# Rows of x gathered ahead for nine half units, their messages made from them later, and a table of counts turned round

## The chip, the cores and the metric

The kernel runs on one core of one Trainium2 chip. The metric is the device time in microseconds (us) of one launch; lower is better. The core has five engines with a queue each: TensorE (PE; PEld are its weight loads), VectorE (DVE), ScalarE (ACT), GpSimd (POOL) and SyncE (SP, which here only issues transfers). Each engine takes its own instructions in order and waits on semaphores.

## The reference, cut to what matters

6250 nodes with 128 features, 100000 edges sorted by `dst`, whose targets crowd at the low numbers. Per edge there are three attention weights, and one message that hangs on the source node alone:

```python
a_k = exp(relu(concat(h[src], h[dst]) @ W_att_k + b_att_k))          # k = 1, 2, 3
avg_a = (a1 / att1[dst] + a2 / att2[dst] + a3 / att3[dst]) / 3.0     # att_k = segment_sum(a_k, dst)
m = avg_a * relu(relu(relu(hs @ W_msg_1 + b1) @ W_msg_2 + b2) @ W_msg_3 + b3)
h_neigh = segment_sum(m, dst) / max(deg, 1)
out = relu(concat(h, h_neigh) @ W_c1 + b_c1) @ W_c2 + b_c2
x = layernorm(x + out)
```

## The kernel before, in words

**Prologue (0 to 54 us).** In 13 chunks of 512 nodes, PE, ACT and DVE make the message of every node (three layers) and its attention logits. A row of 131 words per node (128 of the message, 3 logits) is stored to `message_table` in HBM (`store_rows`). Meanwhile POOL and ACT write zeros into the accumulator `acc` and into `counts`, and no gather is issued, since the table isn't complete.

**The edge pass** then takes the edges in groups of 256 (two tiles of 128). The first 94 groups ("hot" ones, whose targets are the first 384 nodes) need no gather: 24 steps (`COUNT_STEPS`) count for each source node how often it meets each hot target, and 49 later steps (`HOT_AT` + 1 on, one block of 128 source nodes each) turn the counts into weighted sums. The other 297 groups are worked in 126 units: unit 0 of 4 tiles, units 1 to 23 of 8 tiles (the long ones, one beside each counting step), then 102 of 4 tiles (the last of 2). Each tile is gathered from `message_table` by one indirect DMA that POOL issues (L1154), 594 in all, into a ring of 8 places of 4 tiles; POOL may run ahead until the ring is full, and waits on `s_sum` then.

In step i each engine goes through a written order. DVE: `logits_of(i+1)` (L1634, then L1638, which waits until the rows of unit i+1 have landed), `add_counts(i-1)` (L1539, four a step), `one_hots(i)` (L1526, eight a step), `weights(i+1)` (L1646, L1651), `one_hot` (L1592), `add_sums(i-1)` (L1668). PE: `add_edges(i)` (L1281, L1285), `edge_q(i+2)` (L1267), `count_edges(i)` (L1302). ACT: `mask_copy(i+1)` (L1444), `exps(i+1)` (L1404), `low_hots(i)` (L1418, L1423). In a hot step (27 to 75) DVE has three `hot_weights` besides (L1561), ACT three exponentials (L1383) and three biased relus (L1374), PE eighteen matmul records (L1319). All three exponentials go through one bank of PSUM:

```python
act.wait_ge(s_hw, n)                                   # hot_exp: weights n-1 are done with the bank
act.activation(bank[EXP_BANK][0:m, 0:hot_nodes], hot_logit[0:m, n % TWO, :], ACT.Exp)
```

`counts` holds 16-bit counts, [source node in its block, block b, hot target d] with d innermost. `add_counts` adds a window of 6, 9 or 10 targets (`HOT_WIDTHS`, by cells of 32 groups) for all 49 blocks: 49 runs of w elements, in place. `hot_weights` reads the 384 targets of one block: one run.

From step 79 on, the final layers of the nodes (`final_pe`, `final_act`, `final_dve`: L836, L927, ...) lie between the units at places fixed by step numbers.

## Time and profile before

| | |
|---|---|
| time, median of 3 runs | 826.16 us (826.0 to 827.2) |
| the profiled execution: its own time / span | 826.97 / 822.9 us |
| busy: PE / DVE / ACT / POOL | 656.1 / 577.4 / 381.7 / 590.9 us |
| mean granted clock of TensorE | 0.809 |
| gathers on POOL | 594 |

An engine's busy time leaves out waits and the issue of plain transfers. "x" numbers are instructions. A matmul of 32-bit operands shows as two records. A name in brackets behind a row of the timeline is the idle time before it and what ended that. "issue" is idle time that nothing in the profile ended.

### The profile page before, as it was taken

Reading aid. Unit: us, or ns where it says so; the run is one execution under the profiler, and the core shown is the slowest. Engines: PE = TensorE matmul, PEld = TensorE weight load, DVE = VectorE, ACT = ScalarE, POOL = GpSimd, SP = SyncE. Lnnn points to the kernel's source line nnn. Section 1 sums busy time; section 2 is a strip of 40 time slices with the busy share of each in tenths; the row PEclk is TensorE's granted clock in tenths of the full one; section 3 lists DMA queues with packets and bytes.
Section 4 is the critical chain, followed back from the end, with each engine's and each line's share of the span. In section 5 each row is a group of like instructions: output and inputs, shape, how many; then the busy total and the mean of one; then the engine's idle time right before and its main releaser. Section 6 shows DMA issues by size and latency. Waiting matters only on the chain.

```text
span 822.9 us, 16893 instructions
## 1 busy us (share of the span) xinstructions
PE 656.1 (80%) x4917; PEld 512.9 (62%) x4917; DVE 577.4 (70%) x1934; ACT 381.7 (46%) x999; POOL 590.9 (72%) x638
## 2 busy tenths in 40 slices
PE   9945677777578778989898988888877978878885
PEld 5734455544345446778787877776666766667664
DVE  4882656585688877677776767775577868787766
ACT  5522555463444443677676767662123322333323
POOL 7437777777777777777777777777777777777770
PEclk9975555567565675799999999999699989998989
DMA  6533222225652233333333333334233443443421
GB/s 190 142 105 69 63 65 65 65 65 57 71 65 62 62 92 78 74 87 76 80 82 75 83 78 84 77 77 131 65 90 102 112 108 102 104 130 101 98 58 35
DMA packets 79474, 70.44 MB, mean 86 GB/s; under 512 B 34040, under 2 KB 65312, under 8 KB 79376
## 3 DMA queue, kind: packets, MB, share of 16 engines
q0 software_dynamic: 19008, 39.88, 22.2%
q1 hardware_dynamic: 60080, 29.28, 13.3%
q8 instruction: 42, 0.69, 0.3%
q14 instruction: 56, 0.46, 0.2%
q10 hardware_dynamic: 288, 0.13, 0.1%
HBM read 62.32 MB, written 6.90 MB: 84 GB/s over the span
## 4 chain that ended last, share of the span: by engine, by line
POOL 35%; DVE 21%; issue 19%; PE 17%; ACT 4%; DMA 2%; DVEq 2%; ACTq 0%; SPq 0%; POOLq 0%
POOL work L1154 34%; DVE fin L1561 4%; PE bank L1281 4%; DVE acc L1668 3%; ACT bank L1383 3%; DVE counts L1539 2%; DVE fin L1526 2%; DVE fin L927 2%; PE bank L836 2%; PE bank L565 2%; PE bank L544 2%; DMA work<-message_table,src_t 1%; PE bank L1285 1%; PE bank L1319 1%; DVE side L1592 1%
## 5 line engine op out<-in xcount | busy, mean ns | idle before, releaser
L1154 POOL DMA_INDIRECT work<-message_table,src_t x594 | 566.4, 953 | 191.8 <-issue 178.0
L1281 PE MATMUL bank<-work 128*128 128x144 f32 (+8 forms) x1188 | 248.7, 343 | 66.5 <-DVE acc L1668 66.4
L1281 PEld LDWEIGHTS bank<-work 128*128 128x128 f32 x1188 | 197.7, 234 | 100.4 <-issue 86.0
L1444 ACT COPY work<-bank 128x192 f32<-128x192 f32 (+7 forms) x126 | 37.4, 297 | 250.9 <-DVE work L1634 246.5
L1319 PE MATMUL bank<-work,fin 128*128 128x129 f32 (+1 forms) x882 | 117.3, 290 | 0.0
L1668 DVE TENSOR_TENSOR acc<-acc,bank 128x192 f32 (+8 forms) x297 | 88.7, 299 | 31.3 <-issue 7.5
L1319 PEld LDWEIGHTS bank<-work,fin 128*128 128x128 f32 (+1 forms) x882 | 108.2, 201 | 2.5 <-issue 0.6
L1383 ACT ACTIVATE bank<-hot_logit 128x384 f32<-128x384 f32 (+1 forms) x147 | 72.7, 494 | 70.9 <-DVE fin L1561 62.0
L1651 DVE TENSOR_TENSOR work<-bank,work 128x576 f32<-128x576 f32 (+7 forms) x126 | 86.2, 684 | 13.1
L1285 PE MATMUL bank<-work 128*4 128x48 f32 (+8 forms) x1188 | 95.0, 207 | 0.0
L1561 DVE SCALAR_TENSOR_TENSOR fin<-bank,counts 128x384 f32<-128x384 f32 (+1 forms) x147 | 81.4, 554 | 18.1 <-ACT bank L1383 17.4
L1302 PE MATMUL bank<-fin 128*128 128x294 bf16 (+2 forms) x188 | 63.7, 506 | 35.6 <-DVE fin L1526 20.4
L1374 ACT ACTIVATE hot_logit<-logits_or_x,work 128x384 f32<-128x384 f32 (+1 forms) x147 | 88.3, 600 | 0.0
L1638 DVE TENSOR_TENSOR work<-work 128x12 f32<-128x12 f32 (+1 forms) x126 | 22.2, 176 | 80.5 <-DMA work<-message_table,src_t 70.6
L836 PE MATMUL bank<-rest_w,acc 128*128 128x128 f32 x294 | 48.0, 324 | 34.2 <-DVE fin L927 29.3
L1285 PEld LDWEIGHTS bank<-work 128*4 128x4 f32 x1188 | 50.0, 88 | 38.3 <-issue 8.5
L1539 DVE TENSOR_TENSOR counts<-counts,bank 128x294 f32 (+2 forms) x94 | 57.4, 611 | 22.4 <-DVE counts L1539 12.8
L836 PEld LDWEIGHTS bank<-rest_w,acc 128*128 128x128 f32 x294 | 42.4, 227 | 36.5 <-DVE fin L927 30.6
L1302 PEld LDWEIGHTS bank<-fin 128*128 128x128 bf16 x188 | 22.5, 125 | 63.6 <-ACT fin L1423 30.7
L1418 ACT ACTIVATE fin<-fin 128x128 bf16<-128x128 f16 x188 | 59.3, 386 | 1.2 <-PE bank L1302 1.2
L1404 ACT ACTIVATE work<-work 128x12 f32<-128x12 f32 (+1 forms) x126 | 26.8, 213 | 65.4 <-DVE work L1638 63.7
L1646 DVE TENSOR_SCALAR work<-work 128x12 f32<-128x12 f32 (+1 forms) x126 | 24.5, 194 | 41.7 <-ACT work L1404 40.4
(132 smaller groups left out, 688.9 us busy)
## 6 DMA issues: line engine op xcount, KB each, us to landing
work<-message_table,src_t POOLq DMA_INDIRECT x594
side<-near_nodes SPq DMA_DIRECT2D x102, 48.0 KB
side<-logit_parts SPq DMA_DIRECT2D x297, 0.8 KB
message_table<-work SPq DMA_DIRECT2D x12, 262.0 KB, 3.4
work<-message_table SPq DMA_DIRECT2D x48, 65.5 KB
work<-in_x_t SPq DMA_DIRECT2D x12, 256.0 KB, 3.3
fin<-in_x SPq DMA_DIRECT2D x11, 256.0 KB, 2.9
logits_or_x<-in_x_t SPq DMA_DIRECT2D x11, 256.0 KB
```

The lines of the kernel that those rows point to most:

```text
L836: last = pe.matmul(to[:, k * P:(k + 1) * P], acc[:, k, nodes], wc1[:, 1, :], start=True, stop=True)
L1154: pool.indirect_dma_start(out=rows_of(n)[:, t, :], out_offset=None, in_=table[:, :], in_offset=bass.IndirectOffsetOnAxis(ap=src_t[:, h, g: ...
L1281: pe.matmul(sums[:, at:at + HEADS * w], rows_here[:, t, 0:P], wt_of(i)[:, t, :], start=h == 0, stop=h == TILES - 1)
L1285: last = pe.matmul(sums[SUMS_AT:SUMS_AT + HEADS + 1, at + HEADS * w:at + HEADS * w + w], a_col[:, i % THREE, t, :], mask_of(i)[:, t, :], s ...
L1302: pe.matmul(bank[COUNT_BANKS[g % FOUR]][:, 0:n], hot_lo[:, t % HOT_RING, :], hot_comb[:, t % HOT_RING, 0:n], start=h == 0, stop=h == TILES ...
L1319: last = pe.matmul(bank[SIDE_BANKS[h]][:, k * (P + 1):(k + 1) * (P + 1)], hot_wt[0:m, b % THREE, k, h * P:(h + 1) * P], rows_here, start=F ...
L1374: act.activation(hot_logit[0:m, n % TWO, :], hot_ld[0:m, k, :], ACT.Relu, bias=hot_block[0:m, b % BLOCKS, 1 + P + k:2 + P + k]).then_inc(s ...
L1383: act.activation(bank[EXP_BANK][0:m, 0:hot_nodes], hot_logit[0:m, n % TWO, :], ACT.Exp).then_inc(s_he, 1)
L1539: dve.tensor_tensor(here, here, bank[COUNT_BANKS[g % FOUR]][:, 0:w * n_blocks].rearrange("p (b d) -> p b d", d=w), ALU.add).then_inc(s_cad ...
L1561: dve.scalar_tensor_tensor(hot_wt[0:m, b % THREE, k, :], bank[EXP_BANK][0:m, 0:hot_nodes], FLT_MAX, counts[0:m, b, :], ALU.min, ALU.mult). ...
L1651: dve.tensor_tensor(wt_of(i).rearrange("p t (k w) -> p t k w", w=w), from_q(i)[:, :, PARTS:PARTS + w].unsqueeze(2).to_broadcast([P, n, HEA ...
L1668: dve.tensor_tensor(here, here, sums[:, at:at + (HEADS + 1) * w].rearrange("p (k w) -> p k w", w=w), ALU.add).then_inc(s_acc, 1)
```

## The change: what it does

For nine of the long units (4, 6, ..., 20) the second half, two groups, is no longer gathered in the edge pass. In the prologue POOL gathers rows of `x` for them (36 indirect DMAs of 128 rows, three staging buffers), SP stores each half unit to `early_table` in HBM (nine stores) and loads it back in steps 0, 2, ..., 16 (nine loads). The messages of these edges are made then, over two steps and a bit: PE turns the rows (`turn_early`), ACT copies them, PE and ACT run two layers, PE the third, DVE adds the bias into the ring (`rows_early`), ACT applies relu. PE adds the logits of their sources in `edge_q` (four small products). All of it uses bank 3, so that all long units share bank 1 for `edge_q`, which therefore waits for `weights` of the unit just before, and moves behind `count_edges`.

POOL no longer writes zeros for `counts` and for most of `acc`: it writes 5200 words. ACT writes 1000 words per chunk in place of 766, eight late pieces of `acc` (7016 words) behind the prologue's last relu, and the 9408 words of `counts` (five pieces) behind its first `exps`.

`counts` is held with the block b innermost. `add_counts` then touches one run of 49 w elements, and `hot_weights` reads 384 elements that lie 49 elements (98 bytes) apart. The index of the one-hots is made in 6 chained steps in place of 8.

```diff
 
 
 class Straight:
...
+    early_groups = [first_order[n][pair:] for n in early_units]
+    early_a, early_b = early_groups[0][0], early_groups[-1][-1] + 1
+    assert n_hot <= early_a
     columns_most = max(len(u) * TILES * width_of(g) for u in first_order + again_order for g in u)
     assert (HEADS + 1) * columns_most <= 512 * TILES
 
@@ -151,7 +159,7 @@
...
         tally_sum = fin[:, at_index:at_index + max(HOT_WIDTHS)]
         at_index += max(HOT_WIDTHS)
         same = fin[:, at_index:at_index + GROUP // 2].bitcast(bf16)
-        assert at_index + GROUP // 2 <= FIN
...
+        staged = [logits_or_x[:, 0:COLS], work[:, WORK - COLS:WORK], hot_logit_flat[:, 0:COLS]]
+        early_h, early_x, EARLY_BANK = staged[2], staged[1], 3
...
+        ACT_WORDS, POOL_FIRST, POOL_LAST = 1000, 2000, 3200
+        act_from = POOL_FIRST + POOL_LAST
+        late_from = act_from + n_chunks * ACT_WORDS
+        late_pieces = [(a, min(a + ACT_WORDS, n_zeros)) for a in range(late_from, n_zeros, ACT_WORDS)]
+        count_words = hot_nodes * n_blocks // 2
+        count_pieces = [(a, min(a + 2 * ACT_WORDS, count_words)) for a in range(0, count_words, 2 * ACT_WORDS)]
+        zeroed = 2 + n_chunks + len(late_pieces) + len(count_pieces)
...
+                STORE_AT = {0: [0], 2: [1], 3: [2], 5: [3], 6: [4], 8: [5], 10: [6], n_chunks - 1: [7, 8]}
+                assert [k for ks in STORE_AT.values() for k in ks] == list(range(EARLY))
...
+                    sp.wait_ge(s_staged[k % THREE], 16 * CHUNK * (k // THREE + 1))
+                    sp.dma_start(early_table[k * P:(k + 1) * P, :], staged[k % THREE]).then_inc(s_kept[k % THREE], 16)
...
+                    for k in STORE_AT.get(c, []):
+                        store_early(k)
...
+                        a = act_from + c * ACT_WORDS
+                        act.copy(acc_flat[:, a:a + ACT_WORDS],
+                                 zero_col[:, 0:1].to_broadcast([P, ACT_WORDS])).then_inc(s_zero, 1)
...
+                for a, b in late_pieces:
+                    act.copy(acc_flat[:, a:b], zero_col[:, 0:1].to_broadcast([P, b - a])).then_inc(s_zero, 1)
...
-                pool.wait_ge(s_cdve, 2)
-                pool.memset(acc_flat[:, 0:by_pool], 0.0).then_inc(s_zero, 1)
...
+                pool.memset(acc_flat[:, 0:POOL_FIRST], 0.0).then_inc(s_zero, 1)
+                pool.wait_ge(s_early_src, 16)
+                for k, groups in enumerate(early_groups):
+                    if k >= THREE:
+                        pool.wait_ge(s_kept[k % THREE], 16 * (k // THREE))
+                    for j, g in enumerate(groups):
+                        for h in range(TILES):
+                            at = (j * TILES + h) * P
+                            pool.indirect_dma_start(
+                                out=staged[k % THREE][:, at:at + P], out_offset=None, in_=x[:, :],
+                                in_offset=bass.IndirectOffsetOnAxis(ap=src_t[:, h, g:g + 1], axis=0),
+                            ).then_inc(s_staged[k % THREE], 16)
+                pool.memset(acc_flat[:, POOL_FIRST:act_from], 0.0).then_inc(s_zero, 1)
...
+            def q_bank(i):
+                return Q_BANKS[0] if i < n_long else Q_BANKS[i % TWO]
+            def q_user(i):
+                return max((n for n in range(i) if q_bank(n) == q_bank(i)), default=-1)
             def from_q(i):
 
                 n, c = n_tiles(i), PARTS + width(i)
-                return bank[Q_BANKS[i % TWO]][:, 0:n * c].rearrange("p (t c) -> p t c", t=n)
+                return bank[q_bank(i)][:, 0:n * c].rearrange("p (t c) -> p t c", t=n)
...
+                            if j >= pair and early(n) is not None:
+                                continue
...
+                        if k == 0:
+                            for j in range(THREE):
+                                sp.wait_ge(s_kept[j], 16 * len(range(j, EARLY, THREE)))
+                        else:
+                            sp.wait_ge(s_e3, k)
+                        sp.dma_start(early_h, early_table[k * P:(k + 1) * P, :]).then_inc(s_ein, 16)
...
+                        if first and at > 0 and at % EARLY_EVERY == 0 and at // EARLY_EVERY < EARLY:
+                            load_early(at // EARLY_EVERY)
...
-                        if i >= TWO:
-                            pe.wait_ge(s_wt, i - TWO + 1)
+                        if q_user(i) >= 0:
+                            pe.wait_ge(s_wt, q_user(i) + 1)
+                        elif first and q_bank(i) == EARLY_BANK:
+                            pe.wait_ge(s_erow, EARLY)
+                        k = early(i)
+                        if k is not None:
+                            pe.wait_ge(s_ecopy, k + 1)
                         for t in range(n_tiles(i)):
+                            mine = k is not None and t >= CHUNK
                             last = pe.matmul(from_q(i)[:, t, :], near_of(i)[:, t * P:(t + 1) * P],
                                              q_eye[:, slot(i, t // TILES), 0:PARTS + width(i)],
-                                             start=True, stop=True)
+                                             start=True, stop=not mine)
+                            if mine:
+                                last = pe.matmul(from_q(i)[:, t, 0:HEADS],
+                                                 early_x[:, (t - CHUNK) * P:(t - CHUNK + 1) * P], w_logit[:, 0:HEADS],
+                                                 start=False, stop=True)
...
+                        pe.wait_ge(s_ein, 16 * (k + 1))
+                        if k >= 1:
+                            pe.wait_ge(s_erow, k)
+                        for t in range(CHUNK):
+                            last = pe.transpose(bank[EARLY_BANK][:, t * P:(t + 1) * P], early_h[:, t * P:(t + 1) * P],
+                                                ident[:, :])
+                        last.then_inc(s_eturn, 1)
+                    def first_early(k):
+                        pe.wait_ge(s_ecopy, k + 1)
+                        pe.matmul(bank[EARLY_BANK][:, 0:COLS], w1, early_x, start=True, stop=True).then_inc(s_e1, 1)
+                    def second_early(k):
+                        pe.wait_ge(s_eh1, k + 1)
+                        pe.matmul(bank[EARLY_BANK][:, 0:COLS], w2, early_h, start=True, stop=True).then_inc(s_e2, 1)
+                    def third_early(k):
+                        pe.wait_ge(s_eh2, k + 1)
+                        for t in range(CHUNK):
+                            last = pe.matmul(bank[EARLY_BANK][:, t * P:(t + 1) * P], early_h[:, t * P:(t + 1) * P],
+                                             w3[:, :], start=True, stop=True)
+                        last.then_inc(s_e3, 1)
...
+                        if early(i) is not None:
+                            pe.wait_ge(s_emsg, early(i) + 1)
...
-                        if i + 2 < n_units:
+                        if i + 2 < n_units and not (first and i < COUNT_STEPS):
                             edge_q(i + 2)
+                        if k is not None and i % EARLY_EVERY == 0 and k >= 1:
+                            third_early(k - 1)
+                        if k is not None and i % EARLY_EVERY == 1 and k < EARLY:
+                            first_early(k)
                         if first and i < COUNT_STEPS:
                             count_edges(i)
+                        if k is not None and i % EARLY_EVERY == 0 and k < EARLY:
+                            turn_early(k)
+                        if k is not None and i % EARLY_EVERY == 1 and k < EARLY:
+                            second_early(k)
+                        if i + 2 < n_units and first and i < COUNT_STEPS:
+                            edge_q(i + 2)
...
+                    def copy_early(k):
+                        act.wait_ge(s_eturn, k + 1)
+                        if k >= 1:
+                            act.wait_ge(s_q, early_units[k - 1] + 1)
+                        act.copy(early_x, bank[EARLY_BANK][:, 0:COLS]).then_inc(s_ecopy, 1)
+                    def hidden_early(k, layer):
+                        ready, bias, made = ((s_e1, b1, s_eh1), (s_e2, b2, s_eh2))[layer]
+                        act.wait_ge(ready, k + 1)
+                        act.activation(early_h, bank[EARLY_BANK][:, 0:COLS], ACT.Relu, bias=bias).then_inc(made, 1)
+                    def relu_early(k):
+                        act.wait_ge(s_erow, k + 1)
+                        act.activation(early_rows(k), early_rows(k), ACT.Relu).then_inc(s_emsg, 1)
...
+                    if first:
+                        act.wait_ge(s_counts, 1)
+                        act.wait_ge(s_cdve, 2)
+                        words = counts_flat[:, :].bitcast(f32)
+                        for a, b in count_pieces:
+                            act.copy(words[:, a:b], zero_col[:, 0:1].to_broadcast([P, b - a])).then_inc(s_zero, 1)
...
+                        k = early_turn(i)
+                        if k is not None and i % EARLY_EVERY == 0:
+                            if k >= 1:
+                                relu_early(k - 1)
+                            if k < EARLY:
+                                copy_early(k)
+                        if k is not None and i % EARLY_EVERY == 1 and k < EARLY:
+                            hidden_early(k, 0)
+                            hidden_early(k, 1)
...
-                            index(dve.scalar_tensor_tensor(comb_t[:, cell, :], comb_t[:, cell, :], w,
-                                                           dst_t[:, cell, :], ALU.mult, ALU.add))
+                        index(dve.scalar_tensor_tensor(comb_t[:, :, :], dst_t[:, :, :], float(n_blocks),
+                                                       comb_t[:, :, :], ALU.mult, ALU.add))
...
-                            here = counts[:, :, bass.ds(start, w)]
+                            here = counts[:, bass.ds(start, w), :]
                             dve.tensor_tensor(here, here, bank[COUNT_BANKS[g % FOUR]][:, 0:w * n_blocks].rearrange(
-                                "p (b d) -> p b d", d=w), ALU.add).then_inc(s_cadd, 1)
+                                "p (d b) -> p d b", d=w), ALU.add).then_inc(s_cadd, 1)
...
                         dve.scalar_tensor_tensor(hot_wt[0:m, b % THREE, k, :], bank[EXP_BANK][0:m, 0:hot_nodes],
-                                                 FLT_MAX, counts[0:m, b, :], ALU.min, ALU.mult).then_inc(s_hw, 1)
+                                                 FLT_MAX, counts[0:m, :, b], ALU.min, ALU.mult).then_inc(s_hw, 1)
...
+                        if early(i) is not None:
+                            n = CHUNK
+                        dve.tensor_tensor(mine[:, 0:n, :], mine[:, 0:n, :], rows_of(i)[:, 0:n, P:ROW],
+                                          ALU.add).then_inc(s_lg, 1)
...
+                    def rows_early(k):
+                        dve.wait_ge(s_e3, k + 1)
...
+                        dve.tensor_tensor(early_rows(k), bank[EARLY_BANK][:, 0:COLS].rearrange("p (t f) -> p t f", f=P),
+                                          b3_all[:, :].unsqueeze(1).to_broadcast([P, CHUNK, P]),
+                                          ALU.add).then_inc(s_erow, 1)
...
+                        if early_turn(i) is not None and i % EARLY_EVERY == 0 and early_turn(i) >= 1:
+                            rows_early(early_turn(i) - 1)
```

## Rows read from the trace of the kernel before

**Rows 1.** The page: busy us, share of the span, instructions.

```profile
PE 656.1 (80%) x4917; PEld 512.9 (62%) x4917; DVE 577.4 (70%) x1934; ACT 381.7 (46%) x999; POOL 590.9 (72%) x638
```

**Rows 2.** POOL's timeline: first and last gathers of 594.

```profile
54.24 1.11 POOL L1154 DMA_INDIRECT work<-message_table,src_t  x1 [11.12 <-DMA message_table<-work]
55.66 0.95 POOL L1154 DMA_INDIRECT work<-message_table,src_t  x1 [0.30 <-issue]
...
800.37 0.94 POOL L1154 DMA_INDIRECT work<-message_table,src_t  x1 [0.30 <-issue]
```

**Rows 3.** Waits of the whole span, longest first, cut.

```profile
POOL work L1154 <- issue: 178.0, 584, 0.3
...
DVE work L1638 <- DMA work<-message_table,src_t: 70.6, 34, 9.1
```

**Rows 4.** DVE's timeline at L1638: units 1, 14, 23, 125.

```profile
70.74 0.18 DVE L1638 TENSOR_TENSOR work<-work 128x24 f32<-128x24 f32 x1 [7.30 <-DMA work<-message_table,src_t]
...
209.12 0.18 DVE L1638 TENSOR_TENSOR work<-work 128x24 f32<-128x24 f32 x1 [9.06 <-DMA work<-message_table,src_t]
...
298.89 0.18 DVE L1638 TENSOR_TENSOR work<-work 128x24 f32<-128x24 f32 x1
...
805.72 0.17 DVE L1638 TENSOR_TENSOR work<-work 128x6 f32<-128x6 f32 x1
```

**Rows 5.** Windows by stage: busy us of PE, PEld, DVE, ACT, POOL, clock, DMA, GB/s.

```profile
100.00:180.00 80.00, 61.94 (x382) 43.14 (x381) 52.39 (x173) 42.56 (x119) 60.56 (x64) 0.52 0.26 65
...
320.00:560.00 240.00, 214.55 (x1874) 186.37 (x1874) 169.09 (x497) 165.69 (x394) 181.49 (x193) 0.93 0.33 79
```

**Rows 6.** POOL's timeline in the prologue.

```profile
2.81 7.56 POOL L518 MEMSET acc<- 128x8958 f32 x1 [0.91 <-DVE fin L439]
...
42.44 0.68 POOL L528 MEMSET acc<- 128x471 f32 x2 [1.71 <-DVE work L474]
```

**Rows 7.** SP's timeline: chunk 8 and on, then edge pass.

```profile
38.33 6.71 SPq L387 DMA_DIRECT2D message_table<-work  x3
...
47.55 2.84 SPq L387 DMA_DIRECT2D message_table<-work  x3
...
56.64 5.55 SPq L1182 DMA_DIRECT2D side<-logit_parts  x7
```

**Rows 8.** PE's timeline: layers 1, 2, 3 and logits at full clock.

```profile
8.01 1.02 PE L544 MATMUL bank<-work 128*128 128x512 f32 x2
8.87 1.02 PE L553 MATMUL bank<-work 128*128 128x512 f32 x2
...
10.09 0.47 PE L565 MATMUL bank<-rest_w,work 128*128 128x128 f32 x2
10.40 0.28 PE L567 MATMUL bank<-rest_w,work 128*128 128x6 f32 x2
```

**Rows 9.** Timelines of DVE and ACT: a bias add, a zero write.

```profile
36.70 0.68 DVE L494 TENSOR_TENSOR work<-bank,row_b 128x512 f32<-128x512 f32 x1
...
41.71 0.81 ACT L418 COPY acc<-zero_col 128x762 f32<-128x762 f32 x1
```

**Rows 10.** DVE's timeline: adds into counts, targets from 1, 3, 263.

```profile
92.45 0.46 DVE L1539 TENSOR_TENSOR counts<-counts,bank 128x294 f32 x1 [0.20 <-DVE counts L1539]
...
102.45 0.61 DVE L1539 TENSOR_TENSOR counts<-counts,bank 128x294 f32 x1 [0.20 <-DVE counts L1539]
...
291.08 0.81 DVE L1539 TENSOR_TENSOR counts<-counts,bank 128x490 f32 x1 [0.20 <-DVE counts L1539]
```

**Rows 11.** DVE's waits from 320 to 560 us, and L1561 there by form.

```profile
DVE fin L1561 <- ACT bank L1383: 17.1, 48, 0.4
...
DVE work L1638 <- DMA work<-message_table,src_t: 2.7, 5, 1.1
...
L1561 DVE SCALAR_TENSOR_TENSOR fin<-bank,counts 128x384 f32<-128x384 f32 x144 | 79.8, 554 | 17.7 <-ACT bank L1383 17.1 <-PE bank L1319 0.4
```

**Rows 12.** DVE's waits from 560 us to the end.

```profile
DVE work L1638 <- DMA work<-message_table,src_t: 22.0, 14, 4.1
```

100 lines of the change are left out of this document (64 added, 36 removed).

## Prediction

> **What bounds the kernel now.** I first took the page's busy shares [rows 1]. PE is busy 80%, POOL 72%, and no share names the bound. Then POOL's own timeline [rows 2]: the first gather starts at 54.24, the last of 594 at 800.37. That is 746.1 us for 593 steps, 1.258 each; the plain step is 1.25 (0.95 of work and 0.30 of "issue"). In the list of waits POOL has 584 idle gaps of 0.3 us with nothing behind them [rows 3]; it hardly ever waits for a free place in its ring. So POOL works without a pause from the end of the prologue until 5 us ahead of the last unit, and all other engines together keep up with it.
>
> How much faster could they be? The only sign of a starved consumer is DVE's wait for gathered rows at L1638: 34 times, 70.6 us in all [rows 3]. Its place matters [rows 4]. Units 1 to 3 wait 7.30, 6.31 and 1.85 us, and unit 0 0.87: 16.3 us. Units 4 to 13 wait 19.5 us together. Unit 14 waits 9.06, and then DVE does not starve: from unit 14 (209.12) to 23 (298.89) it takes 9.97 us a unit, where POOL offers one each 8 x 1.25 = 10.0. In the hot steps there are waits of 2.7 [rows 11], and behind them 22.0 [rows 12]. The consumer alone, never starved, would need 805.72 - 60.71 - 70.6 = 674.4 us from unit 0 to unit 125. Both sides are thus near one another, and this is what the reader should keep: POOL is the bound, but with only 9% below it.
>
> **POOL's side of the change.** 36 gathers leave the edge pass: 36 x 1.25 = 45.0 us. They must fit into the prologue. There POOL now writes zeros until 43.1 and idles 11.12 us until the table is stored [rows 2, 6]. Zeros cost 7.56 / 8958 = 0.84 ns a word, so 5200 words take 4.4 us. The load of the few indices is second in SP's queue, so I let the gathers start at 5.5: 36 x 1.25 = 45 us give 50.5. A staging buffer must be stored before it is used again; the stores go out behind chunks 0, 2, 3, 5, 6 and 8, one per 7 us at 3.5 us a chunk, where POOL needs one per 5 us of gathers. The last of these, behind chunk 8, goes out at about 42 [rows 7], lands near 46, and the ninth gather set wants it at 45.5: 1 us. With the second write of zeros (2.7 us) POOL is done at 54. So it starts some 1 us later than now.
>
> On SP the last two stores stand ahead of the near-node and logit-part loads of the edge pass; the last one waits for gathers that land near 53. `load_q` moves from 56.64 [rows 7] to about 60, unit 0 by 3 us. But unit 1 waits 7.30 for its rows, which covers it. In the same gap ACT writes its 9408 words: at 0.81 us for 762 [rows 9] that is 10 us by itself, about 8.5 with instructions that overlap, from 61 to 70. It ends where unit 1's exponentials begin (70.9). The eight late pieces, 7.5 us, lie behind ACT's last relu at 49.8 and before its next work at 59.9. I charge the prologue **+1**, bounds 0 and +4.
>
> With 558 gathers left POOL's floor is 55.2 + 558 x 1.25 + the same 5 us of small slips + 1.6 of landing + 2.8: 762 at unit 125, 44 less than now.
>
> **The consumer's side.** Units 1 to 3 stay starved: no early unit is among them. From unit 4 every other unit needs 4 gathers in place of 8, 7.5 us a unit on average, and the consumer is the slower side. The waits from unit 4 on, 70.6 - 16.3 = **-54.3**, can go. A few in the final stage are gaps that another engine would fill: I leave **+3** of them.
>
> New work falls in steps 0 to 18, the stage where I now make the consumer the bound. On DVE: nine bias adds over 512 elements, 0.60 each by spacing (the row of the same shape [rows 9] is 0.68): 5.4. On ACT nine times four passes over 512; ACT is busy 42.6 of 80 us there [rows 5], with room. On PE, at full clock, by the spacing of the prologue's rows [rows 8]: one layer 0.86, twice; layer three and the transposes 4 x 0.31 each; four small logit products 0.6: 4.8 us per half unit, 2.4 a step, and twice that at the lower level of 1.2 GHz. PE is busy 61.9 of 80 us at a granted clock of 0.52 there [rows 5], 7.7 per 10 us step. At 2.4 GHz the same step would be about 4 + 2.4 = 6.4 us of PE in the 8.1 us that the consumer needs unstarved (units 4 to 13: 100.2 us less 19.5, over ten); all of it would be hidden. At 1.2 GHz it is 7.7 + 4.8 = 12.5, and PE is the bound, 4 us above. The stage from 320 to 560, where PE is busy 89%, shows a clock of 0.93 [rows 5]: a fuller PE got the faster level. I take a price per step of 1.2 us in 16 steps (DVE's 0.3 in it, the rest PE and the tighter chain, since `edge_q(i+2)` now waits for `weights(i+1)` and stands behind `count_edges` and the early products): **+19**, bounds +5 and +64. The load of an early half issued behind `third_early` (3 us to land) is covered by `count_edges`, 3.4 us of PE; without it, PE and then `edge_q` wait some 1 us in nine steps.
>
> **The table of counts.** The adds at L1539 lose their 49 short runs. Of the 32 adds of 294 elements, 18 took 0.46 and 14 took 0.61; the groups' lowest targets show that the slower ones start at a target that is 3, 5 or 7 above a multiple of 8, and a start of 263 with 490 elements takes 0.81 where others take 0.67 [rows 10]. One run each should give the lower values: 14 x 0.15 + a few of 0.14 and 0.05: **-3**, all on DVE's path.
>
> The other end is `hot_weights`. L1561 reads counts 98 bytes apart, 147 times, 0.554 each now [rows 11]. It lies wholly on the path of the hot steps: DVE's work, then the exponential that waits for the bank, then DVE again, 4.77 us a unit. No row shows a read with every element in another place. The bounds: nothing, since 49 jumps of 768 bytes per add cost nothing at an even start (0.46 is 294 elements at 1.07 ns, the slope from 0.46 and 0.67 over 196 elements, plus 0.15 as for L1561 itself) [rows 10, 11]; and 0.15 / 49 = 3.1 ns an element from the slow starts, 1.18 us each, +173 us. I take the value of the nearest row of the same table with jumps, **0**, and hold it with little confidence.
>
> The Trainium skill speaks against this: "Vector Engine (DVE) Microarchitecture Reference", section "5.2 Measured stream behaviour on trn2", gives 1.73 ns an element in place of 1.05 when one source jumps at every element, and 2.50 for small steps of 24 words (both sources, or the output). By it 384 elements would cost 0.26 to 0.56 us more, the hot stage 38 to 82, and the sum below would be 831 to 875. The even-start rows don't test it, for their runs are six elements long.
>
> **The sum**, against the profiled execution's 826.97 (0.8 above the median of the three runs): -54.3 + 3 + 1 + 19 - 3 = -34.3, so **793 us**. Unit 125 is at 771; the tail of 21.2 us behind it is unchanged. POOL's floor of 762 lies below it. The likeliest case's own range is 783 to 806.
>
> **The rivals.**
> - *The jumping reads cost about one more slot per element* (slower). Price: 1.07 ns x 384 = 0.41 us, x 147 = +60: 853. For it: every element is a fresh place, unlike any row. Against: the free even starts. It decides from 33 / 147 = 0.22 us an instruction, L1561 at 0.78. From 0.15 to 0.5 us the time is 815 to 866. Chance 0.35. The page's rule above is this rival's first half.
> - *They cost more than 0.5 us each* (the 3.1 ns of the slow starts): 866 to 966. Chance 0.12.
> - *PE becomes the bound of steps 1 to 18 at the lower clock*: 64 in place of 19, 838 us, slower. Against it stands the clock of the fuller stage. Chance 0.08.
> - *POOL stays the bound*: all new work is hidden, 762 + 21 = 779 to 783. The full 45 us are gained but the delay. For it: 34 us of starvation lie in units 4 to 13 and behind 560. Against: 9.97 us a unit without starvation in units 14 to 23. Chance 0.05.
>
> **How the numbers follow.** The forecast has 0.40. From 779 to 862 the range leaves out the heavy jump case and the upper edge of the other, some 0.17 together. A measurement tells 0.2%, 1.7 us, from no change: faster 0.50 (0.40 + 0.05, and 0.05 from jumps under 0.2 us), the same 0.04, slower 0.46.
>
> **What would show it.** L1561: 0.55 right, 0.78 and above wrong; it settles the sign. POOL's first table gather at 55 to 56, 558 of them; POOL now waiting for `s_sum` in gaps of several us from unit 8 or so; L1638's wait for rows down from 70.6 to under 25, most of it in units 0 to 3; the clock in 100 to 180 above 0.52; units 4 to 13 at 8 to 9.5 us each; L1539 at 0.46, 0.61, 0.67 with no second value; the hot steps at 4.8 us. The prediction falls if units 4 to 20 take 11 us or more, if ACT's zeros delay unit 1, or if the hot stage grows.

## Result and the profile after

The changed kernel takes 875.96 us (median of 4 runs, 870.83 to 876.55) where the kernel before takes 826.46: a ratio of 1.0604, 95% interval 1.0583 to 1.0624. It is 6% slower; 793 us were forecast. The profiled execution took 876.47 us with a span of 872.4.

Both ends of the argument show in the page's groups and in the list of waits (busy us, mean ns of one, idle before; then us in total, times, longest):

```profile
PE 705.6 (81%) x5133; PEld 550.1 (63%) x5133; DVE 648.5 (74%) x1941; ACT 419.5 (48%) x1048; POOL 569.5 (65%) x605
...
L1730 DVE SCALAR_TENSOR_TENSOR fin<-bank,counts 128x384 f32<-128x384 f32 (+1 forms) x147 | 143.8, 978 | 17.9 <-ACT bank L1518 17.8
...
POOL work L1224 <- issue: 154.3, 506, 0.4
ACT bank L1518 <- DVE fin L1730: 127.4, 146, 1.7
POOL work L1224 <- PE bank L1409: 101.1, 51, 12.9
```

L1730 is `hot_weights`, L1561 before. One takes 978 ns where it took 554 [rows 11]: +0.424 us, and over the 147 of them +62.4 us (143.8 less 81.4). POOL, which hardly waited for its ring, now waits for it 101.1 us (L1409 is `add_edges`, whose end frees places). And DVE's wait for rows at L1809 (L1638 before), 70.6 us before [rows 3], is 2.6 us. POOL is no longer the bound; the consumer is.

DVE's timeline at L1809 gives the units 1, 4, 14, 24 and 125, as [rows 4] did:

```profile
71.95 0.18 DVE L1809 TENSOR_TENSOR work<-work 128x24 f32<-128x24 f32 x1 [2.34 <-DMA work<-message_table,src_t]
103.44 0.17 DVE L1809 TENSOR_TENSOR work<-work 128x12 f32<-128x12 f32 x1
206.10 0.17 DVE L1809 TENSOR_TENSOR work<-work 128x12 f32<-128x12 f32 x1
318.18 0.17 DVE L1809 TENSOR_TENSOR work<-work 128x12 f32<-128x12 f32 x1
855.49 0.17 DVE L1809 TENSOR_TENSOR work<-work 128x6 f32<-128x6 f32 x1
```

Before, these units came at 70.7, 101.6, 209.1, 307.9 and 805.7. So the changed kernel loses 10.3 us up to unit 24, although 36 gathers are gone from there, and 39.4 us behind it: 537.3 us from unit 24 to unit 125 against 497.9.

The windows from 100 to 180 and from 320 to 622 us (columns as in [rows 5]) show a fuller PE with a higher granted clock, 0.74 for 0.52, and a hot stage in which DVE is the busiest (235.8 of 302 us):

```profile
100.00:180.00 80.00, 75.06 (x476) 53.11 (x476) 51.28 (x172) 50.21 (x134) 50.97 (x54) 0.74 0.27 67
...
320.00:622.00 302.00, 233.45 (x1896) 201.76 (x1894) 235.82 (x519) 164.83 (x394) 202.53 (x215) 0.89 0.28 69
```

### The profile page after: what moved, and what is told of

Same layout as the page of the kernel before. It is cut to its first block, busy times and chain, and to the rows that moved or that the text cites. A ratio compares the mean times of both kernels' runs of the same rounds, so it can differ in the third digit from the quotient of the medians.

```text
span 872.4 us, 17404 instructions
## 1 busy us (share of the span) xinstructions
PE 705.6 (81%) x5133; PEld 550.1 (63%) x5133; DVE 648.5 (74%) x1941; ACT 419.5 (48%) x1048; POOL 569.5 (65%) x605
## 4 chain that ended last, share of the span: by engine, by line
DVE 36%; PE 33%; issue 13%; ACT 9%; DMA 5%; DVEq 2%; SPq 1%; ACTq 0%; POOL 0%
DVE fin L1730 14%; PE bank L1405 11%; ACT bank L1518 5%; DVE acc L1851 4%; PE bank L1409 3%; PE bank L1426 3%; PE bank L881 3%; DMA hot_logit<-early_rows 3%; DVE counts L1708 2%; DVE fin L972 2%; DVE fin L1695 2%; DVE work L1829 2%; PE bank L1379 2%; DVE side L1761 2%; DVE work L1834 1%
## 5 line engine op out<-in xcount | busy, mean ns | idle before, releaser
L1224 POOL DMA_INDIRECT work<-message_table,src_t x558 | 529.5, 949 | 256.5 <-issue 154.3
L1405 PE MATMUL bank<-work 128*128 128x144 f32 (+8 forms) x1188 | 238.3, 332 | 78.8 <-DVE acc L1851 78.8
L1405 PEld LDWEIGHTS bank<-work 128*128 128x128 f32 x1188 | 187.6, 224 | 101.1 <-issue 86.7
L1730 DVE SCALAR_TENSOR_TENSOR fin<-bank,counts 128x384 f32<-128x384 f32 (+1 forms) x147 | 143.8, 978 | 17.9 <-ACT bank L1518 17.8
L1443 PE MATMUL bank<-work,fin 128*128 128x129 f32 (+1 forms) x882 | 129.1, 309 | 0.0
L1443 PEld LDWEIGHTS bank<-work,fin 128*128 128x128 f32 (+1 forms) x882 | 119.7, 219 | 2.3
L1409 PE MATMUL bank<-work 128*4 128x48 f32 (+8 forms) x1188 | 93.8, 205 | 0.0
L1409 PEld LDWEIGHTS bank<-work 128*4 128x4 f32 x1188 | 49.5, 88 | 36.6 <-issue 6.7
L1708 DVE TENSOR_TENSOR counts<-counts,bank 128x294 f32 (+2 forms) x94 | 54.5, 580 | 23.9 <-DVE counts L1708 15.1
L1426 PE MATMUL bank<-fin 128*128 128x294 bf16 (+2 forms) x188 | 55.0, 440 | 18.3 <-ACT fin L1558 10.8
L881 PE MATMUL bank<-rest_w,acc 128*128 128x128 f32 x294 | 47.4, 321 | 23.8 <-DVE fin L972 23.5
L1803 DVE TENSOR_REDUCE work<-bank 128x12 f32<-128x36 f32 (+1 forms) x126 | 24.6, 196 | 48.4 <-PE bank L1357 31.4
L1357 PE MATMUL bank<-side 48*128 48x57 bf16 (+8 forms) x594 | 42.4, 188 | 21.2 <-DMA side<-logit_parts 18.6
```

The lines of the kernel that those rows point to most:

```text
L881: last = pe.matmul(to[:, k * P:(k + 1) * P], acc[:, k, nodes], wc1[:, 1, :], start=True, stop=True)
L1224: pool.indirect_dma_start(out=rows_of(n)[:, t, :], out_offset=None, in_=table[:, :], in_offset=bass.IndirectOffsetOnAxis(ap=src_t[:, h, g: ...
L1405: pe.matmul(sums[:, at:at + HEADS * w], rows_here[:, t, 0:P], wt_of(i)[:, t, :], start=h == 0, stop=h == TILES - 1)
L1409: last = pe.matmul(sums[SUMS_AT:SUMS_AT + HEADS + 1, at + HEADS * w:at + HEADS * w + w], a_col[:, i % THREE, t, :], mask_of(i)[:, t, :], s ...
L1426: pe.matmul(bank[COUNT_BANKS[g % FOUR]][:, 0:n], hot_lo[:, t % HOT_RING, :], hot_comb[:, t % HOT_RING, 0:n], start=h == 0, stop=h == TILES ...
L1443: last = pe.matmul(bank[SIDE_BANKS[h]][:, k * (P + 1):(k + 1) * (P + 1)], hot_wt[0:m, b % THREE, k, h * P:(h + 1) * P], rows_here, start=F ...
```

## The experiments

The experiments ran on five chips, each time with the kernel before beside them. On three of these the kernel before took 987, 996 and 1000 us for 825 on the two others, so times are compared on one chip alone, and across chips only by their ratios to the kernel before. What is common to those three stands at the end of this part. Where several runs share an edit, it is shown once.

**The layout undone, and the layout alone.** Two kernels: the changed one with the old table, and the kernel before with the new one. The edit, from new to old (with the index in 8 steps again):

```diff
-        counts = counts_flat[:, :].rearrange("p (d b) -> p d b", b=n_blocks)
+        counts = counts_flat[:, :].rearrange("p (b d) -> p b d", b=n_blocks)
...
-                            here = counts[:, bass.ds(start, w), :]
+                            here = counts[:, :, bass.ds(start, w)]
...
-                                                 FLT_MAX, counts[0:m, :, b], ALU.min, ALU.mult).then_inc(s_hw, 1)
+                                                 FLT_MAX, counts[0:m, b, :], ALU.min, ALU.mult).then_inc(s_hw, 1)
```

> The changed kernel with the table of counts held as before (target innermost), all else kept. Theory 1 (the jumping reads in hot_weights cost 0.42 us each, 147 times, on the path): L1561's successor falls from 0.98 to 0.55 us, a hot step from 5.9 to about 4.8, and the time by 55 to 62 us, to 814 to 821 us, below the kernel before. Theory 2 (the hot steps are slow for another reason, such as POOL's or the ring's state behind the early units): the instruction gets shorter but the steps stay at 5.5 or more, and the time stays above 845.

Measured: 826.98 us, ratio 1.0014 (0.9988 to 1.0041). The read fell to 0.554 us and a hot step to 4.81, as theory 1 has it, but the time lies 6 to 13 us above the 814 to 821.

> The kernel before with only the table turned round (block innermost), all gathers in the edge pass as before. Theory 1: DVE takes over the bound in the hot steps, 5.9 us a unit against POOL's 5.0; 49 steps give +50 to +55 at unit 76; POOL is then ahead by its ring and the 22 us of waits behind 560 vanish in part, so the time ends at 858 to 868. Theory 2 (POOL's queue hides it): under 840.

Measured: 867.21 us, ratio 1.0504 (1.0477 to 1.0530), within theory 1. So the layout costs 5.9 points of ratio in the changed kernel (1.0604 less 1.0014: 48.8 us) and 5.0 in the kernel before (41.7 us). The rest of the change is worth nothing either way. That is a second miss, since 31 us of gain were forecast for it (54.3 less 19, 3 and 1). In layout_alone the slower hot stage lets POOL run ahead, and part of the 62.4 us comes back as rows that are there in time: DVE's wait for rows falls from 70.6 to 47.4.

```profile
DVE work L1638 <- DMA work<-message_table,src_t: 47.4, 14, 10.8
...
POOL work L1154 <- PE bank L1285: 44.5, 36, 2.0
```

**What a strided read costs.** The changed kernel, in which `hot_weights` reads other places of the same table: block by block the element step runs through 1 to 49 elements of 2 bytes and 1 to 24 words of 4 bytes. The factors are thus not the reference's. It ran once, and only the length of the read is taken from it.

```diff
+                        steps = (1, 2, 3, 4, 6, 8, 12, 16, 24, 32, 40, 48, 49)
+                        words = (1, 2, 4, 8, 12, 24)
...
-                                                 FLT_MAX, counts[0:m, :, b], ALU.min, ALU.mult).then_inc(s_hw, 1)
+                                                 FLT_MAX, of, ALU.min, ALU.mult).then_inc(s_hw, 1)
```

> The changed kernel, its 384-element read of counts in hot_weights replaced by reads of the same table with an element step that goes with the block: 2-byte steps 1, 2, 3, 4, 6, 8, 12, 16, 24, 32, 40, 48, 49, and 4-byte steps 1, 2, 4, 8, 12, 24 (the weights are other numbers then). Theory of the line of 16 bytes: 0.55 us up to a step of 4 elements of 2 bytes (two or more per line), about 0.98 from 8 on. Theory of the 8-byte pair: 0.98 already from 4 on. By the page on the vector engine's streams a step of 24 words costs 1.1 us (2.5 ns an element), a long jump 0.82 (1.73 ns). A flat curve at 0.98 from 2 on would say that any step but 1 costs a second slot.

DVE's timeline at the read, one row each for a step of 1, 6, 8, 32, 48 and 49 elements of 2 bytes (start, duration):

```profile
337.38 0.55 DVE L1737 SCALAR_TENSOR_TENSOR fin<-bank,counts 128x384 f32<-128x384 f32 x1
...
360.64 0.66 DVE L1737 SCALAR_TENSOR_TENSOR fin<-bank,counts 128x384 f32<-128x384 f32 x1
...
365.76 0.83 DVE L1737 SCALAR_TENSOR_TENSOR fin<-bank,counts 128x384 f32<-128x384 f32 x1
...
385.62 0.80 DVE L1737 SCALAR_TENSOR_TENSOR fin<-bank,counts 128x384 f32<-128x384 f32 x1
...
399.47 1.09 DVE L1737 SCALAR_TENSOR_TENSOR fin<-bank,counts 128x384 f32<-128x384 f32 x1
...
405.59 0.97 DVE L1737 SCALAR_TENSOR_TENSOR fin<-bank,counts 128x384 f32<-128x384 f32 x1
```

The 147 reads, us for 384 elements, by step the mean of 6 to 12 of them:

| step in bytes | 2 to 8 | 12 | 16 to 48 | 64 | 80 | 96 | 98 |
|---|---|---|---|---|---|---|---|
| 2-byte elements | 0.56 | 0.67 | 0.82 to 0.85 | 0.80 | 0.94 | 1.10 | 0.98 |
| 4-byte elements | 0.56 | | 0.83 to 0.85 | | | 1.10 | |

Up to 8 bytes apart an element costs what it costs in one run; from 16 bytes on it costs 0.24 to 0.29 us more for the 384, and near 96 bytes up to another 0.27. At the six steps that both widths have (4, 8, 16, 32, 48 and 96 bytes) the two agree within 0.01 us, so the distance in bytes sets the price. Of the theories expected, the 8-byte pair falls, since a step of 8 bytes is free; the line of 16 bytes has the place of the rise right and its size not (0.85 where it had 0.98), and it has nothing for 80 to 98 bytes.

The Trainium skill's table in "Vector Engine (DVE) Microarchitecture Reference", section "5.2 Measured stream behaviour on trn2", which the prediction had named and set aside, gives 1.73 ns an element for one source that jumps 4 KiB at every element, and 2.50 for steps of 24 words in both sources or in the output alone. Here short steps in one source cost (0.82 - 0.15) / 384 = 1.74 ns at 48 bytes, and 24 words in one source alone (1.10 - 0.15) / 384 = 2.47, with the fixed 0.15 us of the prediction. The trace agrees in size, for steps of one source that the table does not list.

**The stores put later.** The changed kernel, with the nine stores of hot logits at steps 18 to 20, behind the last early load, in place of 13 to 15:

```diff
-                    HOT_STORES = HOT_AT // 2
+                    HOT_STORES = EARLY_EVERY * (EARLY - 1) + 2
```

> The changed kernel with the nine small stores of hot logits moved from steps 13 to 15 to steps 18 to 20, behind the last load of an early half. Theory: the step of 16.6 us before unit 16 is PE waiting 5.8 us for that load behind those stores; it falls to about 11, and the gathered units have room then, so the time falls by 4 to 7 us, to about 870. Rival: the stores only move the stall, to the first unit that waits for its gathered rows or its logit parts, and the time stays within 2 us.

Measured: 866.68 us, ratio 1.0509 (1.0482 to 1.0535). That is 0.95 points of ratio or 7.9 us below the changed kernel (the medians, from two occasions, lie 9.3 apart), somewhat more than the 4 to 7 expected. The queues and engines of the changed kernel show why; the load is issued at 220.04, the three stores right behind it:

```profile
220.04 0.35 SPq L1273 DMA_DIRECT2D hot_logit<-early_rows  x1
220.44 1.38 SPq L1305 DMA_DIRECT2D hot_logits<-per_node  x3
...
228.54 1.12 PE L1372 MATMUL bank<-ident,hot_logit 128*128 128x128 f32 x4 [5.76 <-DMA hot_logit<-early_rows]
...
232.43 0.23 DVE L1803 TENSOR_REDUCE work<-bank 128x24 f32<-128x72 f32 x1 [7.08 <-PE bank L1361]
```

The products that need the rows start 8.5 us after the load's issue. With the stores moved, all nine loads land within 2.6 to 3.2 us, and the longest wait of `turn_early` is 1.1 us in place of 5.76. `edge_q` stands behind `turn_early`, and DVE waits 7.08 for the logits of unit 16. The wait also costs clock: PE's four products of 72 columns take 0.67 us ahead of it, at a granted clock of 1.00 (2.4 GHz; 215.5 to 218.6 us), and 1.11 behind it, at 0.50 (1.2 GHz; 228.5 to 240 us).

```profile
218.07 0.67 PE L1405 MATMUL bank<-work 128*128 128x72 f32 x4
...
232.25 1.11 PE L1405 MATMUL bank<-work 128*128 128x72 f32 x4
```

**Both undone, and the price of the early work.** Four kernels with the old layout and the later stores: both_undone has nothing else; no_early_work leaves out all that is computed and loaded for the half units; no_early_old_order besides puts `edge_q` back ahead of `count_edges` with two banks; five_halves is both_undone with `EARLY = 5`, units 4 to 12, and the last store of the prologue its fifth. The last three go by these edits: `return None` in both kernels without early work (also without the loads and waits that belong to it), the line on the banks in no_early_old_order alone (with `edge_q` moved besides), and `EARLY` in five_halves:

```diff
                 def early_turn(i):
 
-                    return i // EARLY_EVERY if first and i < EARLY_EVERY * (EARLY + 1) else None
+                    return None
...
-                return Q_BANKS[0] if i < n_long else Q_BANKS[i % TWO]
+                return Q_BANKS[i % TWO]
...
-EARLY = 9
+EARLY = 5
```

> The old layout of the counts, and the hot-logit stores two steps behind the last early load (steps 18 to 20). Theory A (the two findings add): the early work's collision with the stores cost 9.3 us in the run with the new layout, and 827.0 less 9 is 816 to 820. Rival B (once the layout is undone, the gathers are the bound again in the late part and pace the units at 5.0 each): the 9 us are taken back as new waits, and the time stays at 823 to 827.

Measured: 1022.34 us, 1.0238 (1.0190 to 1.0287) of the kernel before.

> As both_undone, but nothing is computed or loaded for the nine half units (their gathers and their stores in the prologue stay): no turning, no layers, no bias add, no relu, no small logit products, so that the sums take whatever the ring's places hold. The order with edge_q behind count_edges and one bank for it stays. Theory A (the early work itself costs 2.3 us in each of steps 2 to 18): 22 to 35 us below both_undone by unit 24, and then part is given back because the gathers pace the units again; total 785 to 800. Rival B (the single bank and the new place of edge_q cost it, not the work): under 8 us below both_undone at unit 24, total 810 to 818.

Measured: 980.20 us, 0.9835 (0.9782 to 0.9888).

> As no_early_work, with edge_q at its old place ahead of count_edges and the two banks that it had. What is left of the change is 36 gathers fewer and the moved zeros. Theory A: within 3 us of no_early_work. Rival B: 10 or more us below it, with unit 24 some 10 to 15 us sooner. In both, unit 125 can't come before the gathers' floor of 762, so at least 783 in all.

Measured: 973.65 us, 0.9744 (0.9724 to 0.9764).

> As both_undone, with five early half units in place of nine (units 4 to 12; 16 gathers more in the edge pass). If each half unit costs the consumer as much as its four gathers save (5 us), the time is that of both_undone within 2 us. If the early work costs less than it saves, 5 to 10 us slower; if it costs more, that much faster.

Measured: 1007.13 us, 1.0072 (1.0046 to 1.0098).

The same four kernels on a second chip gave nearly the same ratios:

> The kernel of both_undone once more, since on the chip of that call the kernel before took 1000.1 us and the engines stood still in hundreds of gaps that no other run shows. Old layout of the counts, hot-logit stores at steps 18 to 20. Theory A (the two findings add): 816 to 820 where the kernel before takes 825. Rival B (the units are paced at 5.0 each later anyhow): 823 to 827. On the disturbed chip it was 2.4% slower than the kernel before; if that carries over, 845.

Measured: 1011.76 us, 1.0240 (1.0202 to 1.0278).

> The kernel of no_early_work once more: the nine half units are gathered and stored in the prologue, and nothing is loaded or computed for them, so that the sums take whatever the ring's places hold. Theory A (the early work costs 2.3 us in each of steps 2 to 18): unit 24 some 22 to 35 us sooner than in both_undone_2, total 785 to 800. Rival B (the single bank and the new place of edge_q are the cost): under 8 us sooner at unit 24, total 810 to 818. The disturbed chip showed 42 us between the two.

Measured: 972.41 us, 0.9867 (0.9819 to 0.9916).

> The kernel of no_early_old_order once more: edge_q ahead of count_edges with two banks, no early work, 36 gathers fewer. Theory A: within 3 to 7 us of no_early_work_2 (6.5 on the disturbed chip). Rival B: 10 or more us below it. Unit 125 not before 762, so at least 783 in all.

Measured: 964.68 us, 0.9788 (0.9745 to 0.9831).

> The kernel of five_halves once more: five early half units in place of nine. If a half unit costs the consumer what its four gathers save (5 us), the time of both_undone_2 within 2 us; if less, 5 to 10 us slower; if more, faster. On the disturbed chip it was 15 us faster, 3.8 us for each half unit.

Measured: 998.67 us, 1.0121 (1.0066 to 1.0175).

On both chips the early work costs 42.1 and 39.4 us, far more than rival B of no_early_work allows; at unit 24 it is 43.2 and 45.4, more than theory A's 22 to 35 too. Units 4 to 14 take 11.6 to 11.7 us each with the early work and 9.0 to 9.1 without. Four half units fewer make the time 15.2 and 13.1 us shorter, so there each costs more than it saves, part of it in the prologue: unit 0 comes 9.2 and 13.1 us sooner.

The kernels with the new order and one bank are 6.5 and 7.7 us slower than those with the old order, between theory A and rival B. The profiled executions don't show that the order costs this. In the first pair all of the difference is there at unit 4 (142.06 against 132.12), 6 of it before unit 0, and from unit 4 to 24 the two take 194.6 and 195.3 us. In the second pair it lies in one stop of 12.9 us ahead of unit 21, ended by nothing in the core's records. What the order costs thus stays open, but for the step to unit 21 below.

Then three of them, and a fourth kernel, on a chip where the kernel before took 824.8 us:

> The kernel of both_undone a third time, on a chip that is not disturbed if one is to be had: 816 to 820 where the kernel before takes 825 (the two findings add), or 823 to 827 if the later pace of 5.0 a unit takes the gain back. On the disturbed chips it took 1.024 of the kernel before.

Measured: 823.96 us (816.14 to 828.05), ratio 0.9969 (0.9941 to 0.9997). That is the second of the two times; the later pace that it names is taken up in the section on the prediction.

> The kernel of no_early_work a third time (half units gathered and stored in the prologue, nothing loaded or computed for them, the sums take what lies in the ring). If the early work costs 2.3 us in each of steps 2 to 18, unit 24 comes 22 to 35 us sooner than in both_undone_3, and the total is 785 to 800. On the disturbed chips it was 39 and 42 us faster, with units 4 to 14 at 9.1 us each instead of 11.7.

Measured: 798.33 us, ratio 0.9677 (0.9660 to 0.9693). The early work costs 25.6 us in the total and 28.4 at unit 24 (314.75 less 286.38); both this and the total are as expected.

> The kernel of five_halves a third time. On the disturbed chips 13 and 15 us below both_undone, so each half unit cost 3 to 4 us more than it saved. On an undisturbed one: the same time as both_undone_3 within 3 us, if cost and saving are near one another (2.3 x 2 us against 5).

Measured: 817.45 us, ratio 0.9901 (0.9875 to 0.9927). Four half units fewer make it 6.5 us faster, not the same within 3 us: each of the last four costs 1.6 us more than its gathers save.

The fourth takes what waits on PE's queue out of the way of `edge_q`:

```diff
                         if first and i < COUNT_STEPS:
                             count_edges(i)
+                            edge_q(i + 2)
...
-                        if i + 2 < n_units and first and i < COUNT_STEPS:
-                            edge_q(i + 2)
```

> As both_undone (old layout, stores at steps 18 to 20), with edge_q(i+2) directly behind count_edges, so that turn_early, which waits for the load, and second_early, which waits for ACT, stand behind it and no longer hold up the logits of the next unit. Theory A (the place on PE's queue is a good part of the 2.3 us a step): 5 to 15 us below both_undone_3 in the same call, units 4 to 14 at 9.0 to 9.6 us each instead of 10.3. Rival B (PE's time itself, at the lower clock, is the cost): within 3 us of both_undone_3.

Measured: 818.09 us, ratio 0.9924 (0.9902 to 0.9946), 5.9 below both_undone_3 (the two intervals just touch), and unit 24 comes 10.2 us sooner. Units 4 to 14 go from 10.26 us each to 9.79, short of the 9.0 to 9.6 expected, where no_early_work_3 has 8.42: so theory A holds for a quarter of the price there. DVE's waits at the logits' reduce (L1803, here L1802) from 102 to 318 us fall from 24.5 us (16.8 and 7.7) to 14.8:

```profile
DVE work L1802 <- PE bank L1357: 8.5, 5, 3.9
...
DVE work L1802 <- PE bank L1361: 6.3, 6, 1.7
```

From 100 to 180 us PE is busy 74.0 of 80 us in both_undone_3 and 72.0 in queue_order. So PE's own work, rival B, may well be most of the rest; no run separates it.

**The step to unit 21.** It takes 13.2 to 14.0 us in every kernel with the new order (22.6 in no_early_work_2, with the stop named above) and 9.6 to 10.0 in those with the old one. no_early_work_3 shows it without any early work:

```profile
253.66 0.15 DVE L1781 SCALAR_TENSOR_TENSOR more<-least_all,late 1x1 int32<-1x1 f32 x1
...
257.70 0.23 DVE L1792 TENSOR_REDUCE work<-bank 128x24 f32<-128x72 f32 x1 [3.89 <-issue]
...
253.88 3.42 PE L1415 MATMUL bank<-fin 128*128 128x490 bf16 x8 [2.69 <-DVE more L1781]
257.24 0.43 PE L1348 MATMUL bank<-side 48*128 48x37 bf16 x8
```

`count_edges` (L1415) waits there for a word that DVE makes last in its step, `edge_q` (L1348) stands behind it, and DVE has nothing to do until its products are there. Two kernels put `edge_q` ahead of `count_edges` in that one step (on top of queue_order):

```diff
+                        if first and i == LEFT_END:
+                            edge_q(i + 2)
                         if first and i < COUNT_STEPS:
                             count_edges(i)
-                            edge_q(i + 2)
+                            if i != LEFT_END:
+                                edge_q(i + 2)
```

> As queue_order, and in step 19 alone edge_q(21) stands ahead of count_edges(19). Theory: count_edges(19) waits for the word that DVE makes behind weights(20) (L1781 in no_early_work_3), and edge_q(21) stood behind it, so DVE idled 3.9 us; the step to unit 21 falls from 13.25 to about 9.7, the total from 818.1 to 813 to 816. Rival (DVE's own work fills that step, or the late gathers take it back): no change.

Measured: 1016.50 us, ratio 1.0225 (1.0198 to 1.0252). The step to unit 21 took 9.27 us, as expected, but the step after it 12.50 in place of the 8.82 that queue_order had on the quicker chip: 21.8 us for both, where queue_order has 22.1.

> As queue_order_19 with five half units (units 4 to 12). both_undone_3 less five_halves_3 was 6.5 us for four half units, queue_order took 5.9 off nine: if each early half unit still costs more than it saves, 809 to 813, below queue_order_19; if the queue was the whole of the excess cost, 813 to 817, level with it or above.

Measured: 1002.87 us, ratio 1.0059 (1.0046 to 1.0073), 13.6 below queue_order_19: each of the four half units cost more than it saved here too. The step to unit 21 took 11.17, the one after it 12.65, together 23.8 as in five_halves (13.69 and 10.12). Both kernels ran on a chip where the kernel before took 996.3. So the wait was the one named, but the step behind takes back what the one to unit 21 gives. What the move is worth in the total on the quicker chips was not seen.

**The chips on which everything took longer.** Long instructions last as long there (a gather 0.95 us and `hot_weights` 0.556, in both_undone as in both_undone_3), but POOL and DVE stop together for about 1.4 us in nearly every hot step (46 and 47 times in 49), less often elsewhere, and start again together, at something that the core's records do not hold ("remote"). Two rows of both_undone, POOL's and DVE's timelines:

```profile
506.41 0.94 POOL L1224 DMA_INDIRECT work<-message_table,src_t  x1 [1.46 <-remote]
...
506.23 0.20 DVE L1803 TENSOR_REDUCE work<-bank 128x12 f32<-128x36 f32 x1 [1.50 <-remote]
```

A hot step takes 6.1 to 6.2 us in all these kernels, early work or not, and 4.8 in the same kernels on the two quicker chips. What stops them stays open.

## Why the prediction was wrong

**The sum by measured terms.** The ratios to the kernel before, times its 826.46 us: the zeros and the gathers moved, with the new order (no_early_work_3), -26.7; the early work on top (both_undone_3), +24.1; the stores that collide with a load (old_layout less both_undone_3), +3.7, which the totals alone don't prove, for the two intervals overlap, but `turn_early`'s wait of 7.96 us for that load in old_layout is gone in the second, and unit 24 comes 7.8 us sooner; the layout (the changed kernel less old_layout), +48.8. Together +49.9, and 49.5 lie between the medians; that they agree is no check, since each term is the difference between one kernel and the next. The forecast had, for the first line, -54.3 + 3 + 1; for the second +19; for the third nothing; for the last -3 + 0.

**The step that set the sign** is "I take the value of the nearest row of the same table with jumps, 0". L1730 measured 978 ns; the rival "about one more slot per element" named 0.78 and above as the mark, with 0.41 us an instruction, and 0.424 came. Its time of 853 lay below what came because the other half of the forecast failed too. The row that carried the zero does not test it, as the prediction says itself: the adds at an even start have six elements in each run, 12 bytes, and jump once per run, while the read jumps 98 bytes at every element. stride_curve shows that a read is free up to 8 bytes a step and no farther. The layout costs about the same put into the kernel before as it does in the changed one.

**The second failed step** is that "the waits from unit 4 on" can go, -54.3. Behind unit 24 the kernel before already runs at POOL's pace: from there POOL issues its last 393 gathers in 492.5 us (307.85 to 800.37, [rows 2] and the unit's time), 1.253 each. both_undone_3 issues its last 386 from 314.75 to 797.94, 1.252 each; queue_order 387, 1.253 each. All five kernels of the old layout with fewer gathers on the two quicker chips take 488.6 to 490.6 us from unit 24 to unit 125. The early gathers can help there only by what POOL has run ahead at unit 24, and that is bounded by the ring. At unit 24 the kernel before had issued 201 gathers of the 192 needed, both_undone_3 172 of 156: 16 ahead in place of 9, 7 x 1.25 = 8.8 us, and 9.3 were measured. The rest is POOL's wait for the ring, all of it before 320 us except 1.5:

```profile
POOL work L1224 <- PE bank L1409: 46.3, 14, 6.9
```

So the "floor" of 762 at unit 125 was one of a POOL that never waits. With these 46.3 us it is 808, and unit 125 of both_undone_3 came at 803.4. Of the 54.3 us, 24.6 lay behind unit 24 and gave 7 to 9. DVE still waits 10.7 us for rows behind 560. The part in units 4 to 24 was read rightly: 29.7 us of waits lay between 100 and 320, and without early work unit 24 came 21.5 sooner although unit 0 came 6.7 later.

**The third** is the price of the early work, a matter of size. Forecast 19 within 5 and 64; measured 24 to 28 (39 and 42 in the total on the two slower chips), and 4 to 8 more for the collision, which the prediction did not have: it had costed the load as "covered by `count_edges`" from the usual 3 us. The granted clock rose as it had said, from 0.52 to 0.74 from 100 to 180 us. Its reason, that a fuller PE gets the faster level, is not borne out: without the early work the clock was 0.57 with PE busy 72.4 of 80 us. There the consumer, no longer starved, took 8.08 and 8.03 us a unit from unit 4 to 10, the 8.1 of the working. Part of what it cost more is the chain on PE's queue: `edge_q` behind `turn_early` (a load) and behind `second_early` (ACT). queue_order got 5.9 us of it back and lies 19.8 us above no_early_work_3, near the 19 forecast. How that splits between PE's time and ACT's was not separated.

**What held.** The prologue: POOL's first gather from the table at 55.65, as the 55 to 56 said:

```profile
50.83 0.94 POOL L558 DMA_INDIRECT hot_logit<-in_x,src_t  x1 [0.30 <-issue]
51.76 2.79 POOL L562 MEMSET acc<- 128x3200 f32 x1
55.65 0.95 POOL L1224 DMA_INDIRECT work<-message_table,src_t  x1 [1.09 <-DMA message_table<-work]
```

Unit 0 came at 66.1 in place of the forecast 63.7, unit 1 at 71.95, 1.2 later than before. ACT's zeros for `counts` took 8.4 us, as forecast, but from 66.4 to 74.8; the exponentials of unit 1 start behind them at 74.88 in place of 70.95, and DVE waits 1.31 us for them. That sign of being wrong did come, but unit 2 is level with before again (82.01 against 82.07). The adds into `counts` have one value each, by form 463, 616 and 667 ns on average:

```profile
L1708 DVE TENSOR_TENSOR counts<-counts,bank 128x490 f32 x30 | 20.0, 667 | 7.5 <-DVE counts L1708 4.5 <-issue 2.8
...
L1708 DVE TENSOR_TENSOR counts<-counts,bank 128x294 f32 x32 | 14.8, 463 | 7.9 <-DVE counts L1708 5.1 <-issue 2.6
```

Over the 94 adds that is 54.5 us against 57.5: the -3 as forecast, one twentieth of what the same layout costs in the reads. Of the rival "PE becomes the bound" at the lower clock (838), the clock did not come, and on the quicker chips the price was under half of its 64; but PE is busy 75 of 80 us there. Two smaller readings were wrong: the starvation in units 4 to 13 and behind 560 is 19.5 + 22.0 = 41.5 us, not 34, and the six stores behind chunks 0 to 8 lie 5.6 us apart, not 7. Neither enters the sum. "POOL stays the bound" was half true in a way that it did not say: with the old layout POOL is the bound behind unit 24, and the time does not fall to its floor.

The complete versions that come out clearly below the kernel before are queue_order (0.9924) and five_halves_3 (0.9901), by 1% or less and on one chip; on the two slower chips the kernel of five_halves was 0.7% and 1.2% slower than the kernel before, and queue_order was not run there. Both keep the old layout.

## What to carry to other kernels

When a producer with a bounded ring is the bound of a late stage, work taken from it in an early stage comes back only as far as the ring lets it run ahead; count what it has issued ahead at the stage's border, not its total. A layout that turns a few long jumps on the write side into a jump at every element on the read side is to be priced by the bytes between the elements that one instruction reads one after the other, never by rows whose runs are longer. And in an engine's written order, nothing that may wait for a transfer or for another engine's last word should stand ahead of the products that the bounding engine needs next.

## What the runs showed of the hardware that was not expected

A read of DVE costs its full rate up to 8 bytes between elements of 2 or 4 bytes, more at 12 (0.67 us in place of 0.56), 0.80 to 0.85 us from 16 to 64 bytes, 0.94 at 80, 1.10 at 96 and 0.98 at 98, for 384 elements. "Advanced Engine Details and Errata" of the Trainium skill, section "SBUF Cachelines", says that a line has 16 bytes and wants at least two hits; the step at 16 bytes fits that, the one near 96 bytes does not follow from it.

Three stores of 128 x 4 bytes right behind a load of 256 KB on the same engine's queue held up its rows until 8.5 us after its issue, 10.7 in old_layout, where the loads land in 2.6 to 3.2 with the stores moved; moving them gave 7.9 us of time in the changed kernel.

With PE about equally busy from 100 to 180 us, the granted clock, a mean over stretches at its two levels, was 0.57 in no_early_work_3 (PE busy 72.4 of 80 us), 0.73 in both_undone_3 (74.0), and 0.82 in queue_order (72.0).
